# Second attention of a gated cross-attention block: the next batch's tokens turned by DMA with GpSimd's splits, and the last two units turned by TensorE

## The reference

```python
xn = _layernorm(x, gamma_media, beta_media)          # x is ctx_1024 here
ln = _layernorm(latents, gamma_lat, beta_lat)         # latents: _layernorm of the running x
q = ln @ Wq + bq
kv = concatenate([xn, ln], axis=1) @ Wkv + bkv
k, v = split(kv, 2)                                   # 8 heads of 128, 512 keys, 256 queries a batch
q = q * DH ** (-0.5)
attn = softmax(q @ k.T)
x = x + tanh(g_xattn[1]) * ((attn @ v) @ Wo + bo)
```

## Time and profile before

| what | value |
|---|---|
| median of 3 runs | 801.98 us (799.04 to 802.85) |
| the profiled execution | 799.78 us, its span 798.0 us, 1.8 us lie around it |
| stretch of the second attention | about 254.8 to 737 us |
| TensorE busy | 742.0 us, 93% of the span |
| VectorE busy | 675.6 us, 85% |
| ScalarE busy | 515.0 us, 65% |
| GpSimd busy | 267.3 us, 33% |
| DMA | 38.9% of the 16 engines' span by the queue that SyncE and ScalarE feed |

### The profile page before, as it was taken

The page is one execution under the profiler, slowest core; times in us unless marked ns, Lnnn a source line. Parts: engine busy times, 40 slices in busy tenths (PEclk is TensorE's granted clock), DMA queues, the critical chain, the costliest instruction groups (busy, mean ns, idle before and its releaser), DMA issues. The chain is left out here.

```text
span 798.0 us, 14791 instructions
## 1 busy us (share of the span) xinstructions
PE 742.0 (93%) x4888; PEld 595.5 (75%) x4888; DVE 675.6 (85%) x1643; ACT 515.0 (65%) x1103; POOL 267.3 (33%) x375
## 2 busy tenths in 40 slices
PE   5799999998998999999999999999999999995896
PEld 4577777766656787888888888898888888884333
DVE  5778888788887999998998999998988987985697
ACT  4266666676763666666666766676676677664665
POOL 3433333331022133333332332343333323342645
PEclk9699999999999999999999999999999999998899
DMA  4934443320501454445435344444444443452003
GB/s 122 145 124 130 129 130 123 116 88 3 171 1 33 103 93 93 103 104 93 67 69 91 68 78 81 74 82 101 78 85 83 75 72 69 77 97 56 0 1 106
DMA packets 180619, 68.12 MB, mean 85 GB/s; under 512 B 152688, under 2 KB 178864, under 8 KB 180544
## 3 DMA queue, kind: packets, MB, share of 16 engines
q1 hardware_dynamic: 178048, 66.32, 38.9%
q0 software_dynamic: 2496, 0.87, 0.8%
HBM read 17.46 MB, written 2.10 MB: 25 GB/s over the span
## 5 line engine op out<-in xcount | busy, mean ns | idle before, releaser
L1889 ACT ACTIVATE c_pS<-c_pS,c_neg_max 128x512 f32<-128x512 f32 x126 | 83.5, 663 | 122.1 <-DVE c_neg_max L2079 122.1
L1815 POOL CAST c_pT<-c_turned 128x1024 fp32r<-128x1024 f16 x84 | 88.1, 1049 | 176.6 <-PE c_pO L2430 110.9
L2079 DVE TENSOR_REDUCE c_neg_max<-c_pS 128x1 f32<-128x512 f32 x126 | 86.1, 684 | 24.8 <-PE c_pS L2415 24.7
L571 DVE TENSOR_REDUCE a_neg_max<-ab_ps 128x2 f32<-128x512 f32 x128 | 82.4, 684 | 27.4 <-PE ab_ps L818 26.4
L2063 DVE SCALAR_TENSOR_TENSOR c_planes<-c_pS,c_r_sum,c_planes 128x512 f16<-128x512 f32 x126 | 93.4, 741 | 1.5 <-ACT c_planes L1896 1.5
L2430 PE MATMUL c_pO<-c_pT,c_v_hi 128*128 128x256 f32 x504 | 94.2, 284 | 0.0
L410 ACT ACTIVATE a_probsT<-ab_ps 128x512 f32<-128x512 f32 x128 | 69.4, 595 | 29.7 <-PE ab_ps L831 29.2
L1896 ACT ACTIVATE c_planes<-c_pS,c_r_sum 128x512 f16<-128x512 f32 x126 | 86.1, 683 | 1.8 <-DVE c_r_sum L2087 1.7
L2430 PEld LDWEIGHTS c_pO<-c_pT,c_v_hi 128*128 128x128 f32 x504 | 82.6, 190 | 5.5 <-POOL c_pT L1815 0.2
L2399 PE MATMUL c_pV<-w_hi,c_kv 128*128 128x512 f32 x248 | 78.1, 396 | 5.2 <-DVE c_kv L2043 5.2
L2371 PE MATMUL c_pK<-c_kv,w_hi 128*128 128x512 f32 x252 | 78.7, 393 | 1.3 <-PEq L1650 1.3
(11 more groups left out here) (432 smaller groups left out, 1928.4 us busy)
## 6 DMA issues: line engine op xcount, KB each, us to landing
a_q_stack<-w_hi SPq DMA_DIRECT2D x94, 64.0 KB, 2.6
a_k_stack<-w_hi SPq DMA_DIRECT2D x48, 64.0 KB, 2.7
c_kv<-w_hi SPq DMA_DIRECT2D x42, 64.0 KB, 2.6
s_ctx<-in_ctx_dram SPq DMA_DIRECT2D x8, 256.0 KB, 4.0
x_sb<-in_x_dram SPq DMA_DIRECT2D x8, 256.0 KB, 4.5
ctx_in<-in_ctx_dram SPq DMA_DIRECT2D x8, 256.0 KB, 2.9
out_dram<-x_sb SPq DMA_DIRECT2D x7, 256.0 KB, 2.2
c_turned<-c_planes SPq DMA_TRANSPOSE x86, 3.0
```

Source lines behind the costliest of these rows:

```text
L571: nc.vector.tensor_reduce(neg_max[:, r // 2 % 2, e, r % 2, :], pS[:, e, :, :], AX_X, ALU.max, negate=True).then_inc(s["max"], 1)
L1815: nc.gpsimd.tensor_copy(pT[:, :, :, half], turned[n % 3].rearrange("p (a t) q -> p a t q", a=2)).then_inc(s["cast"], 1)
L1889: nc.scalar.activation(unit_bank(n), unit_bank(n), ACT.Exp, bias=neg_max[:, u % 4:u % 4 + 1], accum_out=sums[:, u % 4:u % 4 + 1]).then_inc ...
L2079: nc.vector.tensor_reduce(neg_max[:, u % 4:u % 4 + 1], unit_bank(n), AX_X, ALU.max, negate=True).then_inc(s["max"], 1)
```

## The change

The tokens of the next batch no longer pass through TensorE. They are scaled up by 2^10 in the normalization (`Z_UP`, a factor within `var_eps`), and gamma is divided by it once at the start. GpSimd splits them into two float16 planes (`token_planes`), SyncE turns the planes by a DMA transpose (`turn_tokens`, 256 KB as for a unit's probabilities), GpSimd adds the turned planes (`token_sum`), ScalarE scales and shifts in place (`kv_affine`), and GpSimd makes the high and low parts (`kv_parts`, before on VectorE). The work goes by halves of the tokens (context first, then running x) in place of halves of the features. `turn_kv` is gone, and with it its bank's waits in `project_q`.

The normalization of the tokens of batch b + 2 moves from units 0 to 4 of batch b + 1 to units 8 to 15 of batch b. `bias_in` moves from u = 15 to u = 2 of the batch, out-statistics and `out_normed` to u = 3, 4 and 6; the feed-forward weights' quantization moves to u = 0 of batches 1, 2, 4 and 5, its casts on GpSimd to batches 3 and 5, and its 12 DMA transposes from batches 4 and 5 to batch 6.

In the last batch, the probabilities of the last two units are turned by TensorE (`turn_last`, 4 transposes each) in the score banks, after ScalarE has multiplied them by the reciprocal sum (`normed`). `tail_high` and `tail_low` split them. Head 7's `values` goes to bank `pQ` and right behind head 6's, and the tails are reordered.

```diff
             for b in range(B):
                 for u in range(U1):
-                    turn_probs(U1 * b + u)
+                    if b < B - 1 or u < U1 - 2:
+                        turn_probs(U1 * b + u)
...
+                    if u == (5 if b == 0 else 2) and b + 1 < B:
+                        turn_tokens(2 * b)
+                    if u == (8 if b == 0 else 5) and b + 1 < B:
+                        turn_tokens(2 * b + 1)
...
+            def turn_tokens(i):
+
+                sp.wait_ge(s["zp"], i + 1)
+                wait(sp, s["zsum"], i)
+                sp.dma_start_transpose(z_turned.rearrange("p (a q) -> p a q", q=P), z_planes).then_inc(s["z"], DMA)
...
+            def token_planes(i):
+
+                m, half = i // 2 + 1, i % 2
+                pool.wait_ge(s["latn" if half else "ctxn"], m)
+                wait(pool, s["z"], DMA * i)
+                source = kvn[:, TT:KT, :] if half else ctx_in[:, :, :]
+                nc.gpsimd.tensor_copy(z_parts[:, :, 0, :], source).then_inc(s["zhi"], 1)
+                pool.wait_ge(s["zhi"], i + 1)
+                nc.gpsimd.tensor_tensor(z_parts[:, :, 1, :], source, z_parts[:, :, 0, :], ALU.subtract).then_inc(s["zp"], 1)
+
+            def token_sum(i):
+
+                pool.wait_ge(s["z"], DMA * (i + 1))
+                pool.wait_ge(s["zp"], i + 1 if i % 2 else i + 2)
+                wait(pool, s["kv_lo"], i)
...
+            def kv_parts(i):
+
+                m, half = i // 2 + 1, i % 2
+                high, low = (kv[m % 2][:, y, :, half * T:(half + 1) * T] for y in range(2))
+                pool.wait_ge(s["kvf"], i + 1)
+                nc.gpsimd.tensor_copy(high, kvf).then_inc(s["kv_hi"], 1)
+                pool.wait_ge(s["kv_hi"], i + 1)
+                nc.gpsimd.tensor_tensor(low, kvf, high.bitcast(F32), ALU.subtract).then_inc(s["kv_lo"], 1)
...
+                    elif not last:
+                        if i == 0:
+                            token_planes(2 * b + 1)
+                        if i == 1:
+                            token_sum(2 * b)
+                        if i == 2:
+                            kv_parts(2 * b)
+                            token_sum(2 * b + 1)
+                        if i == 3:
+                            kv_parts(2 * b + 1)
...
+                    if i == 7 and b + 2 < B:
+                        token_planes(2 * (b + 1))
...
-                    if u in (6, 8) and not last:
-                        kv_affine(b + 1, u // 2 - 3)
                     high(n + 2, u + 2)
                     exps(n + 3, u + 3)
+                    if u in ((6, 9) if first else (4, 6)) and not last:
+                        kv_affine(2 * b + (u > (6 if first else 4)))
...
-                    if u in (6, 8) and not last:
-                        kv_parts(b + 1, 1 - par, u // 2 - 3)
...
                 if j == 0:
-                    wait(pe, s["kv_lo"], DC * n)
+                    wait(pe, s["kv_lo"], 2 * n - 1)
+                if j == TT:
+                    wait(pe, s["kv_lo"], 2 * n)
...
+                turn_last(n + 14, 14)
                 turn_x3(b - 1)
+                turn_last(n + 15, 15)
                 out_project(b, 5)
                 values(b, 6)
+                values(b, 7, tail_pT, pQ)
                 out_project(b, 6)
-                values(b, 7, tail_pT)
-                out_project(b, 7)
-                pe.wait_ge(s["x3_sb"], b)
+                out_project(b, 7, *tail_oT)
+                pe.wait_ge(s["oT_lo"], H1 * B)
                 turn_x3(b)
...
-                        if u in (5, 7) and not last:
-                            turn_kv(b + 1, u // 2 - 2)
```

More of the change, by code:

```diff
@@ L1845, in _ @@
[L1845 to L1846 removed]
+                    if b in (3, 5) and i >= 2:
+                        ffn_cast(b // 5, i - 2)
                     if last and i in (1, 3):
                         down_cast(i // 2)
[L1849 to L1853 removed]
@@ L1854, in _ @@
-            last.then_inc(s["cast"], 1)
             power(rstd_o, var_eps_o, "var_o", "rstd_o", B)
@@ L2227, in others @@
                     if u == 6:
+                        out_normed(b - 1)
+                    if u == (8 if last else 9):
+                        out_size(b - 1)
+                    if u == 2 and not last:
                         bias_in(b)
-                    if u == 7:
-                        out_normed(b - 1)
-                    if u == 8:
-                        out_size(b - 1)
-                if u == 1 and not first:
-                    residual(b - 1)
-                if u == 4 and not last:
-                    lat_normed(b + 1)
@@ L2237, in others @@
-                if b + 2 < B:
+                if u == 0 and b in (1, 2, 4, 5):
+                    ffn_whole(b // 4, range(FT // 2) if b in (1, 4) else range(FT // 2, FT))
+                if u == 0 and b == 3:
+                    ffn_row_scales(1)
+                if first and u == 6:
+                    bias_in(0)
+                if last and u == 0:
+                    down_scales()
+                if last and u == 2:
+                    down_whole()
+                if last and u == 7:
+                    bias_in(b)
@@ L2244, in others @@
[L2244 to L2251 removed]
+                        lat_stats(b + 2)
+                        aggregate(b + 2, stats_l, moments_l, var_eps_l, "_l", TT)
+                    if u == 14:
+                        ctx_normed(b + 2)
```

209 lines of the change are left out of this document (103 added, 106 removed).

## The result

The changed kernel took 805.54 us against 801.76 us of the kernel before (medians of 20 runs each): a ratio of 1.0042, 95% interval 1.0028 to 1.0055. It is slower by 0.4%, where 789.1 was predicted and 796.0 was the upper end of the range. By the bound of 0.5% it counts as no change. The profiled execution has a span of 802.5 us, 4.5 more than before.

The account below looks back on a forecast made before the run. TensorE was taken as the bound of the second attention, busy 58.13 of 58.80 us a batch. 6.0 + 4.9 + 2.8 - 0.8 = 12.9 us off the median 801.98 gave 789.1 us, range 784.5 to 796.

Parts of the forecast that it names:

- Two of the prediction's own signs of being wrong: Profile after: TensorE waiting for VectorE's `c_oT_lo` around units 4 and 10 to 15, with `bias_in` above 0.9 us a pair.
- `bias_in` beside GpSimd: `bias_in` in unit 2 collides with GpSimd: 0.8 us lost, bounds a gain of 1 us and a loss of 5.8.
- the rule that the prediction quoted: At `bias_in`: a VectorE instruction with two SBUF inputs and a GpSimd one reading SBUF exclude each other; 0.6 us a pair.
- VectorE "full, but not over": Units 8 to 15 with the moved normalizations: VectorE has 3.3 us of work in a unit's 3.5 us.
- The transposes: 14 turns of the next tokens leave TensorE's stream at 0.43 us each: 6.0 us gained.
- The wait in unit 9: `project_v`'s wait for VectorE's last split of the tokens goes in batches 1 to 6, 0.82 us each: 4.9 us gained.
- The end: Last batch: the last two units need no DMA, so head 7's `values` start right behind head 6's: 2.8 us gained.
- GpSimd's prices: New work on the tokens: 0.77 us a cast, 1.27 a subtraction or sum, 10.7 us a batch.
- The rival of head 3's late casts: GpSimd's four instructions behind head 2 overrun, delaying `values` of head 3 in batches 1 to 6: about 820 us, chance 0.04.
- Batch 0: `kv_affine` of the second half comes late and `project_k` of unit 10 waits: nothing gained, 0 to 2.5 us of waiting possible.
- contention or VectorE as the next bound: Rival: collisions at `bias_in` every batch, or VectorE overfilled in units 8 to 15, take about 5 us: 794, chance 0.16.

Follow-up runs that it names:

- experiment 1: Changed kernel with ScalarE's `kv_affine` moved from between `exps` and `k_high` to behind `q_high` (batch 0 stays in units 6 and 9): 791.68 us.
- experiment 3: Changed kernel with `kv_affine` behind `q_high` and two idle ScalarE instructions of its form in its old place, between `exps` and `k_high`: 798.06 us.
- experiment 4: Changed kernel, VectorE's instructions moved out of GpSimd's way: 784.89 us with `kv_affine` behind `q_high`, 789.55 us with it between `exps` and `k_high`.
- Experiment 6: Kernel before, between `exps` and `k_high` in units 6 and 8: `kv_affine` moved there, 818.67 us; instead two idle ScalarE instructions there, 819.79 us.
- after: The changed kernel with the whole change, against the kernel before: 805.54 us, ratio 1.0042.
- Experiment 8: Kernel before with one transpose of four in each of the 14 turns of the next tokens: 798.26 us, ratio 0.9961.
- experiment 9: Kernel before with the new order of the end alone, the last two units' probabilities turned by TensorE: 799.15 us, ratio 0.9966.

## Why the prediction was wrong

**What failed is what the sum left out: the order on ScalarE.** The diff moves `kv_affine` on ScalarE from ahead of `high` to behind `exps`, right ahead of `k_high`. The prediction named that place for batch 0 only, as the reason why the tokens come late there. It never asked who is queued behind it on ScalarE, and who waits for those. The answer stood in the trace of before: VectorE already waits for `c_k_hi` (6.7 us in 63 instructions), so each step ahead of `k_high` is a step ahead of VectorE. This term, written as nothing, is 13.9 us (experiment 1), and alone the difference between 789.1 and 805.5, but for 2.6 us. It isn't the wait for `k_high` alone: that gave back 6.4 us in experiment 3 and costs 4.7 with VectorE's instructions moved (experiment 4). The rest comes only where VectorE, when it is late, also has instructions that can be lengthened beside GpSimd's splits. Experiment 6 shows that the place is dear without the rest of the change, though there by other waits. Two of the prediction's own signs of being wrong came true: TensorE waits for `c_oT_lo` around unit 4, and `bias_in` takes over 0.9 us.

**`bias_in` beside GpSimd** was the right mechanism in the wrong size. The term was 0.8 us lost: half of 6 collisions, 0.6 us each. In after every one of batches 1 to 6 collides, by 0.9 to 1.6 us (1.79 to 2.45 against 0.87), 1.2 in the mean. (In before two of the eight pairs collided, and not one: that of the last batch took 1.66.) And two instructions that the prediction didn't name collide as well: `out_normed` (1.57 us in the mean, 0.73 alone) and the two-column variance (0.73, 0.17 alone). They have one SBUF input, so the rule that the prediction quoted doesn't cover them. The same section of the Trainium skill ("SBUF — State Buffer", Who interferes with whom) says further that `tensor_scalar` can enter a mode that takes both ports and then contends with GpSimd too. The rows of after agree: 1.59 us instead of 0.73 beside L1859. The prediction weighed only the first half of that rule, although the trace of before held a case of the second: `lat_normed`, which takes 0.73 us for its pair in most batches, takes 1.18 in batch 1 beside a cast.

```profile
347.25 1.04 POOL L1815 CAST c_pT<-c_turned 128x1024 fp32r<-128x1024 f16 x1 [1.99 <-DMA c_turned<-c_planes]
347.67 1.18 DVE L2036 TENSOR_SCALAR c_kvn<-c_kvn,c_moments_l,c_rstd_l 128x256 f32<-128x256 f32 x2
```

By themselves VectorE's instructions in these places cost 2.9 us in batches 1 to 6, inside the bounds (a gain of 1 to a loss of 5.8); beside the late `k_high` they cost 14.0 (355.2 to 341.2).

**VectorE "full, but not over"** was argued for units 8 to 15. It held from unit 9 on: units 10 to 15 are as short as before in batches 1 to 6. But unit 8 takes 4.82 us in the mean of these batches, the longest of all, with lateness that came in units 2 to 6, which the prediction took as relieved. Free time of 5.6 us a batch is no room for a wait of 1.09 and a stretch of 0.86 in the same unit.

**The transposes** (6.0 us): right. Units 5 and 7 lost 0.35 us each in the batches, and units 6 and 8 another 0.12 where nothing else delays them (experiment 1: 3.48 us, 3.60 before). Experiment 8 gave 3.1 for the 4.5 us of three quarters, the rest being waited for in unit 9. **The wait in unit 9** (4.9 us): right, 0.9 us a batch. **The end** (2.8): right, 3.4 in the profile and 2.7 alone. Some of the 3.4 is the clock: where TensorE is at its lower level for some us of the new end too, as it is in before's, the gain is 2.9 to 3.1 (17.3 less 14.2 to 14.4, experiment 9). Head 6's `values` started at 730.79 in after, held by the cast of unit 13; head 7's behind it.

```profile
730.79 0.51 PE L2493 MATMUL c_pO<-c_pT,c_v_hi 128*128 128x256 f32 x2 [0.81 <-POOL c_pT L1831]
736.01 0.75 DVE L2202 SCALAR_TENSOR_TENSOR x_sb<-c_pX,gates,x_sb 128x512 f32<-128x512 f32 x1 [1.08 <-PE c_pX L2506]
```

**GpSimd's prices**: cast 0.77 and two-input 1.27 us were estimated from rows of other forms. They are 0.61 to 0.63 and 1.17 to 1.29, 9.9 us a batch instead of 10.7:

```profile
L1857 POOL CAST c_kv<-c_kvn 128x512 fp32r<-128x512 f32 x14 | 8.6, 615 | 5.1 <-ACT c_kvn L1930 5.1
L1859 POOL TENSOR_TENSOR c_kv<-c_kvn,c_kv 128x512 fp32r<-128x512 f32 x14 | 18.1, 1293 | 1.1
L1849 POOL TENSOR_TENSOR c_kvn<-wd_raw 128x512 f32<-128x512 f16 x14 | 17.2, 1228 | 2.6 <-DMA wd_raw<-wd_raw 1.5 <-POOL c_kv L1859 1.0
L1841 POOL TENSOR_TENSOR wd_raw<-ctx_in,wd_raw 128x512 f16<-128x512 f32 x7 | 8.2, 1169 | 0.6
L1839 POOL CAST wd_raw<-ctx_in 128x512 f16<-128x512 f32 x7 | 4.4, 630 | 11.0 <-DVE ctx_in L2093 11.0
```

The rival of head 3's late casts was rightly held unlikely: only 0.16 us of TensorE's time from unit 0 of batch 1 to batch 7 goes to `c_pT`.

**Batch 0** was written at nothing gained, 0 to 2.5 us of waiting. It lost 3.6: unit 8 takes 6.60 us (4.59 before) and unit 10 5.84 (3.46). `project_k` of unit 10 waits 2.13 us where the prediction had 1.2, and 2.83 us are waited for `c_oT_lo` in unit 8, 0.73 before:

```profile
303.06 0.39 PE L2506 MATMUL c_pX<-c_wo_hi,c_oT_hi 128*128 128x256 f32 x1 [2.83 <-DVE c_oT_lo L2139]
310.39 0.70 PE L2427 MATMUL c_pK<-c_kv,w_hi 128*128 128x512 f32 x2 [2.13 <-POOL c_kv L1859]
```

Among the rivals, "contention or VectorE as the next bound" was the right kind (waits for `c_oT_lo`, `bias_in` stretched), priced at 5 us. In batches 1 to 6 the loss was three times that, 15.3, because the price was worked out as a sum of single collisions, with VectorE on time otherwise.

With the affine behind `q_high` the kernel takes 791.7 us, 2.6 above the forecast. That near miss is in part luck. In batches 1 to 6 the stretched `bias_in` costs more than its term, batch 0 loses 2.0 us where the sum has nothing, while unit 9 gives 5.5 us and not 4.9, and unit 0, for which the sum has no term, 1.2 (3.47 us in the mean, 3.68 before).

## What to carry to other kernels

When a diff moves a step within one engine's order, write down what is queued behind it and which engine waits for that, as carefully as for a wait; the move can cost more than the step. A consumer that waits already, if only for 6.7 us in all as here, is a warning that its producer's order may have no slack. Two small delays of one engine in the same stretch don't add up: alone 1.3 and 2.9 us, together 15.3. And where work goes to GpSimd, list all VectorE instructions of that stretch with two SBUF inputs or of `tensor_scalar`'s kind, and put PSUM readers, reductions and `bn_stats` there instead; none of these was lengthened here. Last, look at the granted clock before a long unit is put down to its wait: in experiment 6 the same wait of 2.29 us was followed by either level.
